# Scatters of a batch cut into 16 pairs along GpSimd's program, and zero fills as pairs behind the second score pass

## The reference

```
xn  = layernorm(x)                                   # x: (16, 512, 256)
q, k, v = xn@Wq.T, xn@Wk.T, xn@Wv.T                  # 16 heads of 16; rope on q and k
attn = softmax(causal(q k^T / 4)) v
logits = xn@router_w.T + bias                        # 32 experts
top 4 of softmax(logits), weights scaled to sum 1
expert(e, t) = (silu(xn@gate_w[e]) * (xn@up_w[e])) @ down_w[e]     # width 128
shared(t)    = (silu(xn@sgate.T) * (xn@sup.T)) @ sdown.T           # width 512
out = x + attn@Wo.T + sum_j w_j expert(e_j, t) + shared(t)
```

## Time and profile before

| | us |
|---|---|
| median of three runs | 2137.58 |
| their range | 2136.33 to 2138.6 |
| span of the profiled execution | 2641.3 |
| PE busy in it | 1935.0 (73%) |
| DVE busy | 1290.2 (49%) |
| ACT busy | 929.5 (35%) |
| POOL busy | 1063.8 (40%) |
| phase A ends in it at about | 1943 |

### The profile page before, as it was taken

How to read it: one execution, slowest core, us unless ns; L and a number is a source line. 1 busy time by engine, 2 the same in 40 slices (tenths; PEclk the granted TensorE clock), 3 DMA queues, 4 the chain that set the end, 5 groups by cost and what they waited for, 6 DMA issues and landing times. The chain is left out here.

```text
span 2641.3 us, 43971 instructions
## 1 busy us (share of the span) xinstructions
PE 1935.0 (73%) x11495; PEld 1234.2 (47%) x11496; DVE 1290.2 (49%) x3379; ACT 929.5 (35%) x1953; POOL 1063.8 (40%) x1056
## 2 busy tenths in 40 slices
PE   5677778787767878777887877874479898998900
PEld 2344444444434444444544444442257777777700
DVE  4445345364534536453453535442235555555567
ACT  2324252443415244242534424341224444444400
POOL 5444343343434334443433444246215544554500
PEclk8888788898878888887988888887689999999955
DMA  5150423415052341505225051432455554545389
GB/s 107 63 97 21 93 40 64 64 40 96 19 94 40 64 64 40 96 22 90 47 57 88 17 100 30 78 59 76 132 158 159 153 150 146 155 144 152 112 304 331
DMA packets 242512, 255.07 MB, mean 97 GB/s; under 512 B 74357, under 2 KB 216190, under 8 KB 242304
## 3 DMA queue, kind: packets, MB, share of 16 engines
q1 hardware_dynamic: 184768, 161.63, 28.4%
q0 software_dynamic: 35840, 71.63, 8.6%
q10 hardware_dynamic: 21824, 20.98, 2.5%
HBM read 112.54 MB, written 94.64 MB: 78 GB/s over the span
## 5 line engine op out<-in xcount | busy, mean ns | idle before, releaser
L745 DVE TENSOR_REDUCE neg<-ps_u 128x2 f32<-128x768 f32 (+3 forms) x384 | 392.4, 1043 | 380.7 <-PE ps_u L952 237.2
L487 POOL DMA_INDIRECT table<-entry,slot x256 | 248.0, 969 | 536.2 <-ACT xs L585 435.4
L982 PE MATMUL ps_u<-we_d 99*128 99x512 bf16 (+3 forms) x1024 | 246.1, 353 | 250.1 <-DMA we_d<-neg_t 121.6
L607 ACT ACTIVATE probs<-ps_u 128x1024 f32<-128x1024 f32 x320 | 323.1, 1027 | 286.6 <-PE ps_u L993 189.2
L1244 POOL DMA_INDIRECT y_dram<-yb,ent x288 | 283.0, 983 | 278.8 <-issue 164.9
L489 POOL DMA_INDIRECT values<-xs,slot x256 | 252.3, 986 | 83.4 <-issue 83.4
L933 PE MATMUL ps_g<-we_gu 128*128 128x512 f32 x512 | 257.7, 634 | 38.1 <-DVE hid L728 32.1
L949 PE MATMUL ps_u<-we_d 96*128 96x128 bf16 (+3 forms) x1024 | 232.2, 312 | 72.4 <-ACT probs L607 26.6
L982 PEld LDWEIGHTS ps_u<-we_d 99*128 99x128 bf16 x1024 | 96.5, 107 | 397.5 <-issue 221.4
L911 PE MATMUL ps_g<-we_gu 128*128 128x512 f32 (+1 forms) x512 | 199.7, 514 | 2.4 <-ACT we_gu L564 2.4
L472 POOL TENSOR_TENSOR rqk<-we_gu 128x512 f32<-128x512 f32 x64 | 81.3, 1270 | 266.2 <-DVE we_gu L709 263.3
(11 more groups left out here) (158 smaller groups left out, 3247.4 us busy)
## 6 DMA issues: line engine op xcount, KB each, us to landing
we_d<-we_gu SPq DMA_DIRECT2D x384, 128.0 KB, 5.9
xg<-values SPq DMA_DIRECT2D x288, 128.0 KB
ys<-y_dram SPq DMA_DIRECT2D x64, 512.0 KB, 5.4
we_gu<-x SPq DMA_DIRECT2D x16, 512.0 KB
xres<-x SPq DMA_DIRECT2D x16, 512.0 KB
sum_dram<-osum SPq DMA_DIRECT2D x16, 512.0 KB, 3.2
we_gu<-wgu_e ACTq DMA_DIRECT2D x16, 512.0 KB
sums_in<-sum_dram SPq DMA_DIRECT2D x8, 1024.0 KB
```

Source lines behind the costliest of these rows:

```text
L487: pool.indirect_dma_start(table[:, :], bass.IndirectOffsetOnAxis(ap=slot[:, k:k + 1], axis=0), entry[:, k, :], None).then_inc(scattered, 16)
L607: nc.scalar.activation(probs[g % 2][:, u, :], ps_u[env[1][step][0]][:, :, :].rearrange("p a n -> p (a n)"), ACT.Exp, scale=SCALE).then_inc ...
L745: nc.vector.tensor_reduce(neg[:, g % 2, i, h0:h0 + nh], src, AX.X, ALU.max, negate=True).then_inc(S["row_max"], 1)
L982: nc.tensor.matmul(ps[:, a, lo:lo + n], k_st[0:MROWS, h, kt * P:(kt + 1) * P], q_st[0:MROWS, h, kt * P:SEQ], start=(lo == 0), stop=False, ...
```

## The change

The 16 pairs of transfers of a batch become 16 steps, `("scat", 0)` to `("scat", 15)`, one pair each. Six stand before the first `qk` step, one between the first and the second, two between the second and the third, one between the third and the fourth, six behind the fourth. Only the first waits for `xs` and `slot`. The 32 fills become 16 steps of two, each behind one named `s2` step of the last batch, and each waits for PE to have finished that step.

```
--- before.py
+++ after.py
-    ("gate", 1), ("s1", 0, 3), ("s1", 0, 4), ("gth", 1), ("scat", 0), ("up", 1), ("lnA",), ("gate", 2), ("s1", 0, 5),
+    ("gate", 1), ("s1", 0, 3), ("scat", 0), ("s1", 0, 4), ("gth", 1), ("up", 1), ("scat", 1), ("lnA",), ("gate", 2),
...
+FILL_AFTER = [(0, 3), (0, 4), (1, 0), (1, 1), (1, 2), (1, 3), (1, 4), (2, 0), (2, 1), (2, 2), (2, 3), (2, 4), (3, 0),
+              (3, 1), (3, 2), (3, 3)]
+FILLS = 2
...
-        if step == ("scat", NT - 1):
-            s.append(("fill",))
+        if step[0] == "s2" and step[1:] in FILL_AFTER:
+            s.append(("fill", FILL_AFTER.index(step[1:])))
...
             def scatter(b, step, env):
-                t = step[1]
-                pool.wait_ge(xs_ready, NT * b + NT)
-                pool.wait_ge(slots, b + 1)
+                k = step[1]
+                if k == 0:
+                    pool.wait_ge(xs_ready, NT * b + NT)
+                    pool.wait_ge(slots, b + 1)
                 hold(pool, passed_pool)
-                for k in range(TOPK * t, TOPK * (t + 1)):
-                    pool.indirect_dma_start(table[:, :], bass.IndirectOffsetOnAxis(ap=slot[:, k:k + 1], axis=0),
-                                            entry[:, k, :], None).then_inc(scattered, 16)
-                    pool.indirect_dma_start(values[:, :], bass.IndirectOffsetOnAxis(ap=slot[:, k:k + 1], axis=0),
-                                            xs[:, k // TOPK, :], None).then_inc(scattered, 16)
+                pool.indirect_dma_start(table[:, :], bass.IndirectOffsetOnAxis(ap=slot[:, k:k + 1], axis=0),
+                                        entry[:, k, :], None).then_inc(scattered, 16)
+                pool.indirect_dma_start(values[:, :], bass.IndirectOffsetOnAxis(ap=slot[:, k:k + 1], axis=0),
+                                        xs[:, k // TOPK, :], None).then_inc(scattered, 16)
 
             def fill(b, step, env):
-                pool.wait_ge(fill_ready, 1)
-                for e in range(E):
+                k = step[1]
+                if k == 0:
+                    pool.wait_ge(fill_ready, 1)
+                pool.wait_ge(pe["s2"], NG * NU2 * (BATCH - 1) + NU2 * FILL_AFTER[k][0] + FILL_AFTER[k][1] + 1)
+                for e in range(FILLS * k, FILLS * (k + 1)):
```

More of the change, by code:

```diff
@@ L75 @@
     ("rankC",), ("gate", 0), ("placeV",), ("s1", 0, 0), ("gth", 0), ("up", 0), ("s1", 0, 1), ("copy",), ("s1", 0, 2),
-    ("gate", 1), ("s1", 0, 3), ("s1", 0, 4), ("gth", 1), ("scat", 0), ("up", 1), ("lnA",), ("gate", 2), ("s1", 0, 5),
-    ("negsplit", 0), ("gth", 2), ("scat", 1), ("s1", 1, 0), ("up", 2), ("s1", 1, 1), ("negT", 0), ("gate", 3),
[11 rows of a table removed]
+    ("gate", 1), ("s1", 0, 3), ("scat", 0), ("s1", 0, 4), ("gth", 1), ("up", 1), ("scat", 1), ("lnA",), ("gate", 2),
+    ("s1", 0, 5), ("scat", 2), ("negsplit", 0), ("gth", 2), ("s1", 1, 0), ("up", 2), ("scat", 3), ("s1", 1, 1),
+    ("negT", 0), ("gate", 3), ("lnB",), ("lnC",), ("gth", 3), ("up", 3), ("scat", 4), ("s2", 0, 0), ("s2", 0, 1),
[9 rows of a table added]
+    ("negsplit", 3), ("route",), ("partsT", 3), ("s2", 2, 4), ("scat", 13), ("negT", 3), ("av", 2, 0), ("av", 2, 1),
+    ("av", 2, 2), ("av", 2, 3), ("s2", 3, 0), ("scat", 14), ("s2", 3, 1), ("avT", 2), ("stack", 0), ("s2", 3, 2),
+    ("s2", 3, 3), ("scat", 15), ("rank",), ("s2", 3, 4),
     ("exps",), ("stack", 1), ("down", 0), ("down", 1), ("rankA",), ("av", 3, 0), ("av", 3, 1), ("av", 3, 2),
```

## The result

On the chip of this comparison the kernel before took 2136.95 us and the changed one 2194.92 us (medians of four runs each): ratio 1.029, 95% interval 1.0264 to 1.0316 (the medians alone give 1.027; one of the four runs after took 2207 us). It is slower by 2.7 to 2.9%; the forecast was 2195 us. These are called the first and the second kind of chip. The profile of before that stands ahead of the prediction, with its span of 2641 us, is of the second kind; the profile after is one of the runs of the first.

The account below looks back on a forecast made before the run. The prediction took the runs as bound by PE, about 86 us a body, with GpSimd perhaps the bound in the last batch. Its terms: 2137.6 + 78 - 21 + 0 = 2195 us, range 2095 to 2255.

Parts of the forecast that it names:

- Placing the 504 us: Profiled span against runs: PE's stall behind transfer rows is nearly all the profiler's, at most 5.5 us a body in runs.
- forecast of 2516 us for the profiled execution: Whole kernel under the profiler: 2641.3 + 78 - 153 - 50, faster although the runs get slower.
- Pairs in the chain, +78 us: Rope chain: four pairs delay adds ACT awaits, so PE loses 5.2 us a body over 15 bodies; bounds 0 and +153.
- Shorter rows, -21 us: Rows before and behind the chain, 16 transfers cut to 12: saves 1.4 us a body; bounds 0 and -82.
- Row before, hold, row behind: Rows on either side of the chain and `hold` writes, 4 to 16 a batch: no gain or cost.
- Fills: Last batch: fills between scatters, 16 new waits for `s2`, up to 10 us GpSimd idle; 0, bounds -20 and +10.
- The port between VectorE and GpSimd: Rope chain: pairs meet DVE casts on a shared port, up to 1 us a body, 15 us, left out of the sum.
- A: Rival: the stall is real in runs and 12 in a row don't hurt; 2085 us, faster; chance 0.22.
- B: Rival: the chain absorbs the pairs and the stall exists only under the profiler; no change, 2138 us; chance 0.08.
- C: Rival: the chain's pairs lie in full on the path, 10.2 us a body, no gain elsewhere; 2290 us; chance 0.12.

Follow-up runs that it names:

- e1_again: The kernel before, unchanged, run again for its profile on a second-kind chip: 2626.45 us without a profile, 2628 with one.
- e5_after: The changed kernel once more, beside the kernel before on a first-kind chip: 2200.3 us, ratio 1.0301.
- e6_slack2: Changed kernel with only two chain pairs, inside tiles where GpSimd waits for ACT; seven ahead, seven behind; first-kind chip: 2118.4 us, ratio 0.9908.
- e7_free2: Changed kernel with all four pairs taken out of the chain, eight ahead, eight behind; first-kind chip: 2141.7 us, ratio 1.0026.
- e9_p23: Changed kernel with only the middle two pairs left in the chain, eight ahead, six behind; second-kind chip: 2547.0 us, ratio 0.965.
- e8_p1: Changed kernel with only the first pair left in the chain, eight ahead, seven behind; second-kind chip: 2572.5 us, ratio 0.9748.
- e10_p4: Changed kernel with only the last pair left in the chain, eight ahead, seven behind; second-kind chip: 2607.9 us, ratio 0.9885.
- e4_scat_only: Changed kernel's scatters, but the 32 fills in one row behind the last scatter, without matmul waits; second-kind chip: 2536.9 us, ratio 0.9663.
- e2_free: Changed kernel with all four pairs taken out of the chain, eight ahead, eight behind; second-kind chip: 2593.9 us, ratio 0.9874.

## Why the prediction was right

The verdict and the median came out as forecast, on a chip of the first kind. On the second kind the same change would be faster by about 5% (the estimate of 2506 us above; with the fills in one row 3.4% faster was measured), and nothing in the prediction tells the two apart: it took the runs' kind for the only one. That the medians agree to the microsecond is luck too, since the terms are off by 3, 1 and 5 us, partly against each other, and a second set gave 2200. Step by step:

**Placing the 504 us: right number, wrong reason.** It was held that the stall belongs to the profiled execution. It goes with the chip: `e1_again`'s unprofiled companions took 2626 us, and the profiled execution of the changed kernel took 2194.87 us where its three others took 2194.63 to 2207.38. No chip was measured at two times, so whether the kind is lasting or a state of that hour isn't shown. The prediction compared a profile from one chip with runs from another without knowing it. The terms for the runs stood all the same, because they were made for a chip without the stall. The forecast of 2516 us for the profiled execution failed by that step (2193.0 measured); the estimate for a chip with the stall is 2506. The Trainium skill (NOTIFIC — the notification-queue block, 7.1) says that inside its block a record backs up rather than gets lost, so that the path can throttle an engine. By the runs above tracing cost nothing that the spread of the runs doesn't cover.

**Pairs in the chain, +78 us: held.** Measured 75 us between `e5_after` and `e6_slack2`, 5.0 instead of 5.2 us a body. In the trace of the profile after, PE comes 0.3 us late at the first step (forecast 0.4), 1.7 at the second (2.5 cumulated) and 4.3 at the third (5.2). The adds start 2.2, 3.8 and 4.3 us late instead of 2.3, 4.6 and 5.2: the second tile's 483 ends 0.6 and not 1.2 us late (its wait for ACT shrank from 3.84 to 2.23 us), and the later adds inherit that. The middle two pairs cost PE 1.5 us there and not 2.1, the last 2.5 as against 2.7. PE's waits by ACT are where they were looked for: 1.30 and 2.67 us, 64.1 in all, against 0.9 in `e7_free2`.

**Shorter rows, -21 us: held in size, not in mechanism.** It was a quarter of a loss that could not be placed, so the agreement is luck. What the traces show is a late landing: in `e7_free2` the last of 16 transfers releases VectorE 9 us after GpSimd was done with it, 1.49 us too late for the next `entry`, and one pair fewer takes nearly all of it away (18.4 to 1.3 us); with rows of 12, in `e5_after`, VectorE doesn't wait at all. That this wait is the cause of the 20 us is inferred from the two traces; the runs made to isolate it fell on chips where it doesn't occur.

**Row before, hold, row behind: nothing, as said.** No row of waits that was read shows a cost for any of them; none was tested by itself.

**Fills: forecast 0 (-20 to +10).** `e7_free2`, which differs from the kernel before in the fills and their waits and in 16 instead of 4 writes of `hold`, took 5 us more (3 to 8); which of these edits costs it was not tested on the first kind of chip. GpSimd idles before the first fill, as the prediction feared, though 6 us and not 10:

```profile
1433.68 0.99 POOL L505 DMA_INDIRECT values<-zeros,fill_row  x1 [6.13 <-PE ps_u L1003]
```

On the chips with the stall the same edit gained 30 us.

**The port between VectorE and GpSimd: up to 15 us feared, nothing lost.** The cast that stood beside an addition met it less often, not more: this second cast took 410 ns on average before and 189 after.

```profile
L766 DVE CAST neg_p<-neg_r 128x16 bf16<-128x16 f32 x64 | 12.1, 189 | 2.2
```

It is the two pairs ahead of the third tile that part them, on both kinds of chip: the same row of `e7_free2`, with none, and that of `e9_p23`, with these two alone:

```profile
L766 DVE CAST neg_p<-neg_r 128x16 bf16<-128x16 f32 x64 | 26.7, 416 | 2.2
```

```profile
L766 DVE CAST neg_p<-neg_r 128x16 bf16<-128x16 f32 x64 | 11.8, 184 | 2.2
```

It stays at 413 and 422 ns in `e8_p1` and `e10_p4`. The collision that the Trainium skill (SBUF — State Buffer, Who interferes with whom) describes, where one of the two is blocked for the other's whole instruction, needs both to overlap in time. The trace agrees: in the earlier trace rows the cast ends with the addition, at 353.44 against 353.41 us.

**The rivals.** A needed a stall that is real and costs less with 12 in a row than with 16. Both are true where before takes 2626 us, and `e4_scat_only` is 3.4% faster there; it fails where the stall is absent. B is excluded by 64.1 us of PE waiting for ACT, C by PE being 4.3 and not 10.2 us late. The terms as measured, 2137 + 75 - 20 + 5 = 2197, come near 2195 and 2200, but this is no second proof: they are the steps from the kernel before by `e7_free2` and `e6_slack2` to `e5_after`, and must end there.

## What to carry to other kernels

When the profiled span and the timed runs lie as far apart as here (504 us of 2138), suspect two chips before the profiler, and time the unchanged kernel where it is profiled before pricing anything that the gap touches. Transfers issued by GpSimd are not free between the links of a chain that another engine waits for in order: here the last pair of 2.55 us cost PE 2.5 us, since ScalarE already idled for the add behind it, and pairs in a gap where GpSimd itself waits for ScalarE cost nothing that the trace shows (2118 us against 2200 on one chip). A long row of them may cost by the late landing of its last, so look for who reuses its source buffer.

## What was not expected of the hardware

Two kinds of chip: the same kernel takes 2137 us on some (two sets here, mean granted clock 0.94) and 2626 to 2640 on others (three sets, 0.85 to 0.86). On the latter, ACT, VectorE and PE sit idle behind rows of back-to-back indirect transfers by nothing that the profile names, ACT and VectorE for up to 20 us at a time in the loop, until shortly after the row is issued (in `e2_free` the row ends at 318.7 us and ACT goes on at 321.4); a row of 12 on each side costs 109.5 - 90.8 = 18.7 us a body in all, one of 16 costs 115.5 - 87.2 = 28.3. What sets a chip's kind was not found, nor whether it lasts.
